# Seven interleaving transfers per attention, an early Gelu at the turn's end, and new places for the light steps in a fused four-layer attention kernel

## The reference, cut to what matters

```python
def layer0(ctx, x):                      # one wide head, no projections
    n = norm(x); c = norm(ctx)
    h = gelu(attention(n, c, c) @ fc1.T + b1)
    cross = h @ fc2.T + b2
    return n + gamma2 * (cross + gamma1 * attention(norm(cross)))
def layer1(x, ctx):                      # linear attention with elu, then a norm
    ...
def layer2(x, ctx):
    x = x + mha(norm(x), norm(x))        # SELF2, 16 heads of 8
    x = x + mha(norm(x), norm(ctx))      # CROSS2
    h = norm(x)                          # 8 experts of 512, two of them weighed per token
    gates = softmax(top2(h @ router.T + rb))
    return x + sum(gate_e * (gelu(h @ fc1_e.T + b1_e) @ fc2_e.T + b2_e))
def layer3(x, ctx):
    x1 = norm(x + attention16(x, x, causal) @ Wo_s + bo_s)      # SELF3
    x2 = norm(x1 + attention16(x1, ctx) @ Wo_c + bo_c)          # CROSS3
    return norm(x2 + relu(x2 @ W1 + b1) @ W2 + b2)
```

## Time and profile before

| | us |
|---|---|
| median of 3 runs | 2806.71 |
| lowest, highest | 2804.61, 2808.42 |
| the profiled execution | 2807.83 |
| its span, first to last instruction | 2805.6 |
| PE busy in it | 2378.3 (85%) |
| DVE, ACT, POOL busy | 1531.1, 1520.5, 551.7 |

### The profile page before, as it was taken

How to read it: one execution, slowest core, us unless ns; L and a number is a source line. 1 busy time by engine, 2 the same in 40 slices (tenths; PEclk the granted TensorE clock), 3 DMA queues, 4 the chain that set the end, 5 groups by cost and what they waited for, 6 DMA issues and landing times. The chain is left out here.

```text
span 2805.6 us, 69952 instructions
## 1 busy us (share of the span) xinstructions
PE 2378.3 (85%) x27712; PEld 1659.8 (59%) x27712; DVE 1531.1 (55%) x4449; ACT 1520.5 (54%) x2379; POOL 551.7 (20%) x730
## 2 busy tenths in 40 slices
PE   3656989898989989897989989898989989888975
PEld 2334647575666757575666657575766657564643
DVE  3343555657465565657465665656465565635232
ACT  1324555665656565665656655665666565645432
POOL 2111112121212122122212222121212122111111
PEclk9655989999999999999999999999999999998975
DMA  2100010101010110101010110111010111110000
GB/s 113 34 16 13 23 29 19 33 23 45 24 44 24 29 29 24 33 24 44 23 44 24 31 31 21 31 26 42 23 44 24 33 29 24 28 29 17 17 20 17
DMA packets 103753, 84.22 MB, mean 30 GB/s; under 512 B 15001, under 2 KB 102682, under 8 KB 102938
## 3 DMA queue, kind: packets, MB, share of 16 engines
q1 hardware_dynamic: 103449, 79.91, 11.6%
HBM read 14.21 MB, written 4.19 MB: 7 GB/s over the span
## 5 line engine op out<-in xcount | busy, mean ns | idle before, releaser
L992 DVE TENSOR_REDUCE smax<-by_query_banks 128x8 f32<-128x616 f32 (+1 forms) x512 | 516.3, 1008 | 351.0 <-PE by_query_banks L1309 350.4
L778 ACT ACTIVATE probs<-by_key_banks 77x1024 f32<-77x1024 f32 (+1 forms) x480 | 485.5, 1011 | 165.9 <-PE by_key_banks L1332 162.6
L1246 PEld LDWEIGHTS by_key_banks<-moe_w,hid 128*128 128x128 f32 x4096 | 476.0, 192 | 14.1
L1246 PE MATMUL by_key_banks<-moe_w,hid 128*128 128x128 f32 x4096 | 483.7, 275 | 0.0
L759 ACT ACTIVATE hid<-by_query_banks,cols 128x512 f32<-128x512 f32 x512 | 334.7, 687 | 268.5 <-PE by_query_banks L1237 266.7
L1380 PE MATMUL weighed_bank<-probs,values 128*32 128x128 f32 x8192 | 361.6, 299 | 4.9 <-ACT o_sb L783 2.7
L1309 PE MATMUL by_query_banks<-k_int,q_int 32*128 32x128 f16 (+1 forms) x4096 | 199.8, 220 | 168.8 <-DVE smax L992 87.3
L1309 PEld LDWEIGHTS by_query_banks<-k_int,q_int 32*128 32x128 f16 x4096 | 121.6, 99 | 335.7 <-issue 219.6
L1380 PEld LDWEIGHTS weighed_bank<-probs,values 128*32 128x32 f32 x8192 | 209.1, 116 | 97.6 <-issue 46.3
L772 ACT ACTIVATE m_sb<-turned_bank 16x128 f16<-16x128 f32 x256 | 67.9, 265 | 297.5 <-PE turned_bank L1362 297.4
L1332 PE MATMUL by_key_banks<-q_int,k_int 32*128 32x128 f16 x3840 | 208.8, 232 | 9.2 <-ACT probs L778 7.0
(11 more groups left out here) (238 smaller groups left out, 3915.1 us busy)
## 6 DMA issues: line engine op xcount, KB each, us to landing
q_int<-q_nat SPq DMA_DIRECT2D x256, 128.0 KB, 2.7
k_int<-k_nat SPq DMA_DIRECT2D x128, 128.0 KB, 2.7
k_int<-k_nat SPq DMA_DIRECT2D x128, 77.0 KB, 2.3
x_tok<-in_x SPq DMA_DIRECT2D x17, 256.0 KB, 3.1
q_int<-m_sb SPq DMA_DIRECT2D x256, 4.0 KB
out<-res SPq DMA_DIRECT2D x16, 256.0 KB, 2.7
ctx_tok<-in_ctx SPq DMA_DIRECT2D x17, 154.0 KB
hid<-in_moe_w SPq DMA_DIRECT2D x1, 2048.0 KB
```

The lines of the kernel that those rows point to most:

```text
L778: act.activation(probs[h % 2][0:nk], pair[0:nk], ACT.Exp, scale=DH ** -0.5)\
L992: dve.tensor_reduce(smax[h // 2 % 2][:, pair, :], scores, AX.X, ALU.max, negate=True)\
L1246: last = pe.matmul(B[e % 2][:, seq_tok(b)], hidden[e % 2][:, c, seq_tok(b)], moe_w2[:, e, c, :], start=(c == 0), stop=(c == CHUNKS - 1))
```

## The change

1. The features of the key and query projections are put in another order (`spread`, on the host, once), so that one transfer of 128 partitions fills one of the four rows of all four tiles. There are seven for each attention: keys high twice, keys low, queries high twice, queries low, and a short one that sets the queries' spare rows back to zero from a constant tile `lines`. Four are issued at `proj` and three at `query`, the high ones when ACT is done and the low one when DVE is. The constant rows of the keys are filled at the start, by four of eight transfers that stand between the weights and the experts' weights; PE waits for them before its first instruction.
2. The copies on POOL (`twice`) are gone. PE waits for one semaphore, `shift`, of all seven, at the first scores of an attention. 
3. ACT runs a Gelu on a tile of 128 x 4 (`early`) behind the query projection of CROSS2, at the end of each turn.
4. `TURNS` is a new table, and the steps it moves are moved by one to a few heavy steps.

```diff
 TURNS = {
-    "PE": "iiiiiihxlhhxxxllhlhllhhllhxlhlhllhhxhhlhhllxhhhlhlhhllhhlllhhhhxxxhhhhhhxhxhxhhhhhhxhhhhhhhhhhxh"
+    "PE": "iiiiiihxlhhxxxllhlhllhhllhxlhlhllhhxhhlhhllxhhhlhlhhllhhlllhhhhxxxhhhhhhxhxhxhhhhhhxhhhhhhhhhhhx"
...
 }
...
-           o_sb=BLOCKS, o_t=BLOCKS, o_rden=BLOCKS, o_norm=BLOCKS, proj=3, proj_sb=3, low=2, dup=2,
+           o_sb=BLOCKS, o_t=BLOCKS, o_rden=BLOCKS, o_norm=BLOCKS, proj=3, proj_sb=3, low=2,
...
-PER |= {f"shift_{j}": 2 * 16 for j in range(TILES)} | {f"m_shift_{j}": 16 for j in range(TILES)}
+PER |= dict(shift=7 * 16) | {f"m_shift_{j}": 16 for j in range(TILES)}
...
-        k_nat = sb("k_nat", [P, PARTS, N], F16)
-        q_nat = sb("q_nat", [P, PARTS, N], F16)
+        k_nat = sb("k_nat", [P, 2, N], F16)
+        q_nat = sb("q_nat", [P, 2, N], F16)
+        lines = sb("lines", [P, 2, N], F16)
...
+            sp.wait_ge(s_fill, 2)
+            for m, x in enumerate(att):
+                sp.dma_start(x.k_int[3::PARTS, :, :], lines[:, 0, 0:GROUP * KEYS[m]]).then_inc(s_lines, 16)
+                sp.dma_start(x.q_int[3::PARTS, :, :], lines[:, 1, :]).then_inc(s_lines, 16)
...
                 yield f"proj{m}"
+                sp.wait_ge(S["proj_sb"], at(g, "proj_sb", 1))
+                sp.dma_start(x.k_int[0::PARTS, :, :], k_nat[:, 0, 0:keys]).then_inc(S["shift"], 16)
+                sp.dma_start(x.k_int[2::PARTS, :, :], k_nat[:, 0, 0:keys]).then_inc(S["shift"], 16)
+                sp.dma_start(x.q_int[3::32, :, :], lines[0:16, 1, :]).then_inc(S["shift"], 16)
                 sp.wait_ge(S["low"], at(g, "low", 1))
-                sp.wait_ge(S["dup"], at(g, "dup", 1))
-                sp.dma_start(x.k_int[:, 0, :], k_nat[0:32, :, 0:keys]).then_inc(S["shift_0"], 16)
+                sp.dma_start(x.k_int[1::PARTS, :, :], k_nat[:, 1, 0:keys]).then_inc(S["shift"], 16)
                 yield f"query{m}"
+                sp.wait_ge(S["proj_sb"], at(g, "proj_sb", 2))
+                sp.dma_start(x.q_int[0::PARTS, :, :], q_nat[:, 0, :]).then_inc(S["shift"], 16)
+                sp.dma_start(x.q_int[1::PARTS, :, :], q_nat[:, 0, :]).then_inc(S["shift"], 16)
                 sp.wait_ge(S["low"], at(g, "low", 2))
-                sp.wait_ge(S["dup"], at(g, "dup", 2))
-                sp.dma_start(x.q_int[:, 0, :], q_nat[0:32, :, :]).then_inc(S["shift_0"], 16)
-                for j in range(1, TILES):
-                    sp.dma_start(x.k_int[:, j, :], k_nat[rows_of(j), :, 0:keys]).then_inc(S[f"shift_{j}"], 16)
-                    sp.dma_start(x.q_int[:, j, :], q_nat[rows_of(j), :, :]).then_inc(S[f"shift_{j}"], 16)
+                sp.dma_start(x.q_int[2::PARTS, :, :], q_nat[:, 1, :]).then_inc(S["shift"], 16)
...
-                pool.tensor_copy(k_nat[:, 2, 0:keys], k_nat[:, 0, 0:keys]).then_inc(S["dup"], 1)
...
-                pool.tensor_copy(q_nat[:, 1, :], q_nat[:, 0, :]).then_inc(S["dup"], 1)
...
                 act.activation(q_nat[:, 0, :], X[0][:], ACT.Identity, bias=col(f"bq{m}")).then_inc(S["proj_sb"], 1)
+                if m == CROSS2:
+                    act.activation(early[:], ln_eps[:], ACT.Gelu)
...
-                    if c % 2 == 0:
-                        pe.wait_ge(S[f"shift_{j}"], at(source, f"shift_{j}"))
+                    if c == 0:
+                        pe.wait_ge(S["shift"], at(source, "shift"))
...
+            pe.wait_ge(s_lines, 16 * 2 * len(att))
...
+    spread = np.arange(D).reshape(TILES, D // TILES).T.reshape(-1)
+    for m in range(4):
+        for w in "qk":
+            mat[f"w{w}{m}"] = mat[f"w{w}{m}"][:, spread]
+            col[f"b{w}{m}"] = col[f"b{w}{m}"][spread]
```

More of the change, by code:

```diff
@@ L132 @@
-    "SP": "iiiiiillllllxxxxxhhhhhhhhhhhhhhhhhhhhhhhhhhhhhhhhhhhhllllllllllllllllxxxxxxhhhxhhhhhhhhhhhxxxhhh"
-          "hhhhhhhhhhhhhhhhhhhhhhhhhhhhhxxxxxxxxxxxxxxxxxxxhhhhhhhhhhhhhhhhhhhhhhhhhhhhhhhhhhhhhhhhhhhhhhhh"
-          "hhhhhhhhhhhhhhhhhhhhhhhhhhhhhhhxxxxxxxxx",
+    "PE": "iiiiiihxlhhxxxllhlhllhhllhxlhlhllhhxhhhlhllxhhhlhlhhllhhlllhhhhxxxhhhhhhxhxhxhhhhhhxhhhhhhhhhhhx"
+          "hhhhhhhhxhhhhhhhhxhhhhhhhhxhhhhhhhhxhhhhhxxxhhhhhhhhhhhhhhhxhhhhhhhhhhxhhxhhhhxhxxxhhhhhhhhhhhhh"
+          "hhxhhhhxhhhhxxxxhhxhxxhhhhhhhhhhxhhxxxxh",
@@ new lines @@
+    "ACT": "iiiihxxxxhhllllhhhhllllhxlhhlhllhxhhhllhlllhhhhhhhxllllhlhhhhhhhhhhhhiixxxxxhhhxhhhhxhhhhhhhhhhh"
+          "xhhhhhhxhhhhhhhhhhxhhhhhhxhhhhhhhhhhxxxxhhhhhhhhhhhhhhhhhhhhhhhhxxhhhhhhhhhxxhhhhxxhhhxhhhhhhhhh"
+          "hhhxhhhhxxxxhhhxxxxhhhhhhhhhhhhhhxxhhxxx",
+    "DVE": "lllxhxhhhxxhllhxlllllilhhhhxllhhhhhhhhillhhllhlhhhlllhhlxxxhhhxhhxhhhhhhhhhxhhxxxhhhhhhhhhhhhhhh"
+          "hhhhhhhhxhhhhhhhhxxhhxhhhhhhhhhhhhhhhhhhxxhhhhhhxhhhhhhhhhhhhhhxhhhhxhhhxxhhhhhxxhhhhhhhhxxxhhhh"
+          "hhhhhhhhhhhhhxhxhxxxhhhxxxiiihhhhhxxxxhi",
@@ L314, in build @@
         minus_half = sb("minus_half", [P, GROUP])
+        early = sb("early", [P, GROUP])
         self_scale = sb("self_scale", [P, D])
@@ L427, in build @@
                  (ctx_tok[:, :, D:], 1.0), (v0[:, :, 4:], 1.0), (h[:, :, 4:], 1.0), (cross_hat[:, :, D:], 1.0),
-                 (ln_eps[:], LN_EPS), (minus_half[:], -0.5), (k_nat[:, 3, :], MAX_SCALE), (q_nat[:, 3, :], 0.0)]
+                 (ln_eps[:], LN_EPS), (minus_half[:], -0.5)]
+        fills = [(lines[:, 0, :], MAX_SCALE), (lines[:, 1, :], 0.0)] + fills
         fills += [(x.v_wide[:], 0.0) for x in att] + [(p[:], 0.0) for p in probs]
@@ L593, in light @@
                     pool.tensor_tensor(res3[:], res3[:], shifted(shift31), ALU.add).then_inc(S["res31"], 1)
-                    yield from twice(r, CROSS3)
                 yield "value3"
@@ L617, in light @@
                     pool.tensor_tensor(x_sa[:], x_sa[:], row("sa_out_b"), ALU.add).then_inc(S["sa_res"], 1)
-                    yield from twice(r, SELF2)
                 if r.b:
@@ L622, in light @@
                     pool.tensor_tensor(x_s3[:], x_s3[:], row("bo_s"), ALU.add).then_inc(S["s3_res"], 1)
-                    yield from twice(r, SELF3)
                 if r.f:
@@ L642, in light @@
                     pool.tensor_tensor(x_ca[:], x_ca[:], row("ca_out_b"), ALU.add).then_inc(S["ca_res"], 1)
-                    yield from twice(r, CROSS2)
                 if r.t:
@@ L727, in project @@
                 if not g.first:
-                    for j in range(TILES):
-                        act.wait_ge(S[f"shift_{j}"], at(g.before(), f"shift_{j}"))
+                    act.wait_ge(S["shift"], at(g.before(), "shift"))
                 act.wait_ge(S["proj"], at(g, "proj", 1))
@@ L963, in low_parts @@
                 dve.wait_ge(S["proj_sb"], at(g, "proj_sb", 2))
-                dve.scalar_tensor_tensor(q_nat[:, 2, :], X[0][:], col(f"bq{m}"), q_nat[:, 0, :],
+                dve.scalar_tensor_tensor(q_nat[:, 1, :], X[0][:], col(f"bq{m}"), q_nat[:, 0, :],
                                          ALU.add, ALU.subtract).then_inc(S["low"], 1)
```

26 lines of the change are left out of this document (7 added, 19 removed).

## The result

The changed kernel takes 2862.8 us (median of 4 runs, 2855.4 to 2867.6) against 2807.6 us (2804.6 to 2809.0). The ratio is 1.0196, with a 95% interval of 1.0172 to 1.0220: about 55 us slower, where 2809 us was forecast and 2786 to 2822 us given. The profiled execution is the one of 2863.37 us, with a span of 2861.6.

The account below looks back on a forecast made before the run. PE, with its waits and its clock, was taken to bound the kernel. From the profiled 2807.8 us, -2.1 + 2.5 + 1.5 gave 2809.7; with the runs' median 1.1 lower, 2809 us was forecast, range 2786 to 2822.

Parts of the forecast that it names:

- What bounds the kernel: Whole kernel: PE, busy 85% of the span, bounds it; time is gained only where PE itself stops waiting.
- Step 2, the copies on POOL: Keys' and queries' copies on GpSimd: never the last wait, so removing them gives 0 us, 0.1 at most.
- Step 5, the light pieces: Light PE work behind weighings in the loop: 0 to 0.35 us late, 0.18 taken; +2.5 us over 14 turns.
- The slower rival: Light pieces behind weighings delay ACT's exponentials: 7 us, plus 9 from more 159.2 us turns; 2823 or 2814 us; chance 0.22.
- the other moves ... where nobody waits: 0: Other table moves, such as normalised hat ahead of an expert's sum on DVE and gap_exp ahead of o_sb: 0.
- Step 3, seven transfers: Seven transfers for eight per attention: free in the loop, 0.5 us later at three bare waits, +1.5 us (0 to 3).
- the rival of 2800 us: SyncE's shorter queue and earlier low parts shorten the heads' chain by 0.5 us a turn, 7 us; chance 0.08.
- Step 1, the early Gelu: Table load before the experts hides in ACT's idle time; gates' copy 0.14 us sooner, 2.1 us less over 15 turns.
- The rivals of 2787 and 2767 us: Experts' table load fully on the path, 2787 us, chance 0.14; its drain goes too, 2767 us, chance 0.02.
- Step 4, the constant lines: Eight start transfers, about 1 MB, land by 13.5 or 15 us, before PE starts at 17.36: 0, at worst +2.
- Some tenths may be evened out: Loop turns: tenths won or lost in a turn may be evened out; the mean should stay near 157 us.
- a rival of another kind, at 2773 us: Clock drop behind the first scores disappears, each turn 154.6 instead of 157.0 us, 34 us less; chance 0.08.

Follow-up runs that it names:

- experiment 18: Kernel of 8 with POOL's 128 copies back, into a spare tile that no transfer reads: ratio 0.9965 to the kernel before.
- experiment 1: Changed kernel with one wait added on POOL, holding res back until CROSS2's q_nat is written: ratio 1.0040 to the kernel before, 2817.2 us.
- experiment 4: Kernel before with POOL making the result's two additions ahead of CROSS2's two copies: ratio 1.0215, 2868.0 us.
- 14: Kernel of 8 with SELF3's query product behind the weighing on PE and q_nat ahead of an exponential on ACT: ratio 0.9988 to the kernel before.
- 13: Kernel of 8 with SELF3's value product moved behind the weighing on PE: ratio 0.9996 to the kernel before.
- experiment 10: Kernel of 8 with PE's string of the new table alone: ratio 1.0054 to the kernel before.
- 12: Kernel of 8 with DVE's string of the new table alone: ratio 1.0007 to the kernel before.
- 8: Changed kernel with POOL's added wait and the table of the kernel before for all five engines: ratio 0.9969 to the kernel before, 2792.1 us.
- 5: Kernel before with the early Gelu alone: ratio 1.0001.
- 4 to 7: Four edits of the kernel before; the one not listed singly moves DVE's ctx_hat steps ahead of hat: ratio 0.9981.
- 2: Changed kernel with DVE's order among the layers as in the kernel before: ratio 1.0221 to the kernel before.
- 3: Changed kernel with DVE's order among the layers as before and POOL's added wait: ratio 1.0035 to the kernel before.
- 7: Kernel before with DVE's ctx_hat ahead of hat and PE's last turning back ahead of the value product: ratio 0.9995.
- 17: Changed kernel with two unread products of 1.02 us right behind CROSS2's query product, in PE's wait for k_nat: ratio 1.0333 to the kernel before.
- run 30: Not a run's label: the text reads "a median run 30 us slower", a time difference, for the changed kernel with two unread products: ratio 1.0333.

## Why the prediction was wrong

- **What bounds the kernel: right in kind.** PE's time decides, and the loss came by its waits and its clock. But the reading went by instructions on the way to PE and took each as long as in the trace. That `ctx_hat` took 2.06 us for four steps, one of 1.30 and three of 0.33, stood in the trace of before and was not asked about. It was the warning.
- **Step 2, the copies on POOL (0 us): this step failed.** That the copies themselves are never waited for is right (experiment 18). What they held back was not looked at: behind them in POOL's queue stood `res`, and nothing was said of when it would run then and beside what. It costs 28 us of wait on PE and, with what follows, 46 us when undone (1) and 61 when brought about (4).
- **Step 5, the light pieces (0.18 us a turn, +2.5 us): one piece sized too low, the others left out.** The move that was walked works as walked, at the top of its bounds: 0.34 us a turn, about 5 us (14). But "PE's own sum is unchanged, since both stand between the same pairs of scores" leaves out that PE waits between them, at the value product for the bank that `o_sb` empties, and that the piece filled this wait: 0.57 us a turn, 8 us (13). The whole string costs 24 us (10), and how much of it is clock was not foreseen. The slower rival (7 us, or 16 with more two-drop turns) came nearer, and its late exponential is what the query product shows.
- **Step 5, DVE's sums (in "the other moves ... where nobody waits: 0"): wrong.** The prediction doesn't name the experts' sums that now stand ahead of `p` and `x_phi`. Such a sum has to wait for its own product, and `x_phi` waits behind it. 11 us (12).
- **Step 3, seven transfers (+1.5 us): wrong sign.** Of the bare waits the one in the tail went from 3.35 us to 3.39, not to 3.85, the first from 2.87 to 3.98, and the third, of 0.78, is gone. PE's list now has 14.3 us under the queries' transfers, in 15 waits, but 13 of these stand in the loop and are at most 0.64 us long; in the kernel before PE waited as long there, and its list puts that down to ACT's exponential. A full-clock turn is 0.5 us shorter, and 0.3% is won in all (8, 18), which lies near the rival of 2800 us. Which step of the chain brings it is not shown.
- **Step 1, the early Gelu (-2.1 us): right in kind, and smaller.** The load hides in ACT's idle time as walked; PE's wait for the gates' copy fell from 0.84 to 0.81, not by 0.14, and nothing is left in the runs (5). The rivals of 2787 and 2767 us are out.
- **Step 4, the constant lines (0, at worst +2): near the bound.** PE starts at 19.2 instead of 17.36 us, because the weights themselves land at 13.00 instead of 11.13. The start also varies from run to run: 17.4 to 18.8 us in the profiled runs of the kernel before and of 4 to 7, 18.3 to 20.4 us in those with the lines.
- **The clock.** "Some tenths may be evened out" is what 2, 3 and 7 show. But the mean did not stay at 157, and the clock isn't neutral: with PE's products unchanged, new orders moved its busy time in the profiled runs by 24 us (1), 37 us (4) and 42 us (10). The prediction had this only as a rival of another kind, at 2773 us.

The ledger of a turn, all from rows or twin instructions: +2.06 (28 us over the run) for the collision, +1.36 (19 us) for DVE's sums, about +0.83 (12 us) for PE's pieces (tenth kernel against eighth, in two turns with the same drops), -0.5 (7 us) for the transfers, +1.9 once at the start. That is 54 us, beside 55 measured. That the sum fits so well is in part luck: taken singly in the runs the three are worth 46, 11 and 24 us, with POOL's wait the two strings together cost only 20, and 21 of the 56 us by which the span grew are busy time of PE.

**What stays open** is why a kernel settles at more or less time at 1.2 GHz. The kernel before was run more than 110 times beside the experiments, with a mean clock of 0.916 to 0.928, and a straight line through these runs, which scatter widely about it, falls by 10.6 us for each 0.01 of clock. By that, 12 us of the 61 of experiment 4 and 12 of the 24 of experiment 10 would be clock (0.917 against 0.928), and 5 or 6 of the 46 of experiment 1; the busy times of the profiled runs give it more. So the share of the clock is not settled. It is also not shown what sets the drops; filling PE's long wait did not help (17).

## What to carry to other kernels

When an instruction is taken out of a queue, look at what stood behind it there: it will start sooner, and the question is beside what. A light step can't be moved past a heavy one for nothing, even where nobody waits for its result: ask which idle time it fills now, and that can be a wait for a bank as well as for data. And an instruction whose duration has two values in the trace (0.33 and 1.30 us for the same shape) shows a contention that already exists and that any reordering can multiply.

## What the hardware did that was not expected

- A DVE `TENSOR_SCALAR` of 77 x 128 f32 from and to SBUF takes 0.33 us alone and 1.28 to 1.31 us when it starts within the first 0.1 us of a POOL sum or product of 128 x 512 f32 (1.26 to 1.31 us): it then ends 0.08 to 0.09 us behind the end of that one, in all 29 such cases of the changed kernel. It isn't DVE at large that is slowed: the same operation with its input in the matrix engine's banks, `cross_hat`, takes 0.40 us beside a large POOL step (12 cases) and without one (52), and `x_s`, whose product comes from the matrix engine's banks, stays at 320 to 353 ns in all 512 cases, 78 of them beside a POOL step of 128 x 512:

```profile
L974 DVE SCALAR_TENSOR_TENSOR x_s<-by_key_banks,gates,x_s x512: 320/342/353, 294.4 to 2717.3; 128x128 f32<-128x128 f32 x171
```

  The Trainium skill has the rule (SBUF — State Buffer, "SBUF: two separate sides"): VectorE and GpSimd share a pair of SBUF ports, which is "an exclusive lock, not a bandwidth split".
- Two products of 1.02 us each, put into a wait of PE where they delay nothing in the profiled run, went with a median run 30 us slower than without them (2893 against 2863 us; ratios 1.0333 and 1.0196), at a median clock of 0.907 against 0.921. Why is not shown: the one profiled run of the six was the fastest, 2857 us at 0.926.
- The order of a few instructions alone moved how long PE was busy with the same 27712 products: 2378.3 us before, 2415.0 with two steps and two copies of POOL exchanged, at a clock of 0.920 and 0.906.
